# GpSimd's order in an attention period: low halves behind the routing's copy and at step 16, outputs spread over steps 10 to 21

## What is computed

```python
x = _layernorm(x + _L0_attn_ref(x, ...))  # a scan over time and an MLP
x = _layernorm(x + _L0_ffn_ref(x, ...))   # 8 experts, the 2 best of each token
x = _layernorm(x + _L1_attn_ref(x, ...))  # attention, 16 heads of 8, q and k normalised
x = _layernorm(x + _L1_ffn_ref(x, ...))   # 4 experts, each an attention over its own tokens
```

## Time and profile before

| | |
|---|---|
| time, median of 3 runs | 1452.36 us (1451.96 to 1455.44) |
| profiled execution: span from first to last instruction | 1481.8 us (no other time of it is given) |
| PE busy | 1231.5 us, 83% |
| DVE busy | 964.4 us, 65% |
| ACT busy | 734.6 us, 50% |
| POOL busy | 663.4 us, 45% |
| mean granted clock of PE | 0.878 |

### The profile page before, as it was taken

The page is one execution under the profiler, slowest core; times in us unless marked ns, Lnnn a source line. Parts: engine busy times, 40 slices in busy tenths (PEclk is TensorE's granted clock), DMA queues, the critical chain, the costliest instruction groups (busy, mean ns, idle before and its releaser), DMA issues.

```text
span 1481.8 us, 30563 instructions
## 1 busy us (share of the span) xinstructions
PE 1231.5 (83%) x11664; PEld 742.3 (50%) x11664; DVE 964.4 (65%) x2280; ACT 734.6 (50%) x1244; POOL 663.4 (45%) x1054
## 2 busy tenths in 40 slices
PE   5878786567667889999998998999899888988985
PEld 2555575455223344555555554555555455555543
DVE  4787532255357887777776868677777766757534
ACT  3654432233342456665665656556565554553531
POOL 3376342563167454464443626345363432443430
PEclk7998798797665889999998989999999998998978
DMA  9801465561010001101020110101102010110110
GB/s 337 335 21 34 133 184 161 166 181 54 19 29 23 23 2 40 29 16 38 8 44 8 37 32 13 44 4 42 32 14 43 4 42 15 31 39 9 34 35 8
DMA packets 69480, 87.52 MB, mean 59 GB/s; under 512 B 22062, under 2 KB 54104, under 8 KB 65880
## 3 DMA queue, kind: packets, MB, share of 16 engines
q1 hardware_dynamic: 65240, 77.18, 18.0%
q0 software_dynamic: 4096, 8.40, 1.9%
HBM read 52.16 MB, written 32.21 MB: 57 GB/s over the span
## 4 chain that ended last, share of the span: by engine, by line
PE 41%; DVE 28%; SPq 7%; ACT 7%; issue 6%; POOL 5%; DMA 3%; another core or an unknown queue 2%; ACTq 0%; DVEq 0%; POOLq 0%
PE ps L1677 19%; DVE mneg_e L1492 8%; PE ps L1757 7%; PE ps L864 5%; PE ps L1780 3%; DVE mneg_l L1492 3%; SPq L1141 2%; PE ps L960 2%; SPq L1137 2%; DVE q L1547 1%; PE ps L972 1%; SPq L1159 1%; POOL q_low L1224 1%; PE ps L1777 1%
## 5 line engine op out<-in xcount | busy, mean ns | idle before, releaser
L1335 ACT ACTIVATE probs<-ps 128x1024 f32<-128x1024 f32 x384 | 390.0, 1024 | 260.8 <-PE ps L1677 257.2
L1492 DVE TENSOR_REDUCE mneg_e<-ps 128x2 f32<-128x512 f32 x512 | 337.1, 685 | 66.1 <-PE ps L1677 63.1
L1677 PE MATMUL ps<-k_high,q_high 32*128 32x256 f16 x1024 | 164.3, 286 | 51.0 <-DVE mneg_e L1492 41.1
L1492 DVE TENSOR_REDUCE mneg_l<-ps 128x2 f32<-128x512 f32 x256 | 167.8, 682 | 57.3 <-PE ps L1677 56.1
L1757 PE MATMUL ps<-probs,v_e 128*32 128x256 f32 x2048 | 141.6, 395 | 8.2 <-ACT v_e L1360 4.7
L1677 PE MATMUL ps<-q_high,k_high 32*128 32x256 f16 x1024 | 142.1, 278 | 4.0 <-ACT probs L1335 3.3
L1677 PE MATMUL ps<-q_low,k_high 32*128 32x256 f16 x1024 | 141.4, 275 | 0.0
L1677 PE MATMUL ps<-q_high,k_low 32*128 32x256 f16 x1024 | 140.3, 273 | 0.0
L1677 PE MATMUL ps<-kT,qT 32*128 32x256 f16 x512 | 75.9, 285 | 35.6 <-DVE mneg_e L1492 16.7
L1677 PEld LDWEIGHTS ps<-k_high,q_high 32*128 32x128 f16 x1024 | 54.4, 93 | 97.4 <-DVE mneg_e L1492 62.8
L1288 POOL TENSOR_TENSOR on_e<-o_e,on_e 128x512 f32<-128x512 f32 x60 | 75.7, 1274 | 60.1 <-DMA on_e<-scratch_e 60.1
(11 more groups left out here) (245 smaller groups left out, 2553.6 us busy)
## 6 DMA issues: line engine op xcount, KB each, us to landing
by_expert<-expert_w SPq DMA_DIRECT2D x12, 1536.0 KB, 14.4
expert_w<-in_expert_w SPq DMA_DIRECT2D x48, 321.0 KB
on_e<-scratch_e SPq DMA_DIRECT2D x60, 256.0 KB, 4.8
tokens<-by_expert SPq DMA_DIRECT2D x48, 128.0 KB
by_expert<-y_tokens SPq DMA_DIRECT2D x48, 128.0 KB
on_l<-scratch_l SPq DMA_DIRECT2D x128, 32.0 KB, 1.8
sums_l<-o_l SPq DMA_DIRECT2D x128, 2.0 KB
q_high<-shiftT_e SPq DMA_DIRECT2D x128, 2.0 KB
```

Source lines behind the costliest of these rows:

```text
L1335: act.activation(probs[:, probs_slot(r, i)].rearrange("p j s -> p (j s)"), s_banks(i).rearrange("p j s -> p (j s)"), ACT.Exp, scale=0.5 if ...
L1492: v.tensor_reduce(to, tiles(max_bank(k)), axis=AX, op=ALU.max, negate=True).then_inc(kind.max_used, 1)
L1677: return pe.matmul(o, l, r, start=start, stop=stop)
```

## The change

GpSimd's conditions are put in another order. In period `r`, the low halves of groups 2 and 3 of sequence `r` move from step 5 (both of group 2), 6 and 7 to step 6 behind the copy `routeT16` (both of group 2), step 7 (`q` of group 3) and step 9 (`k` of group 3). The low halves of group 1 of sequence `r + 1` move from steps 20 and 21 to step 16, ahead of `on_l`. The four multiplications `on_e` move from steps 9, 10, 11 and 12 to steps 10, 13, 17 and 21. SP waits at steps 4 and 9 for the low halves of the two groups whose `q_high` row it is about to write. DVE takes `inverse_l` at step 13, no longer at step 12. No operation is added or left out.

```diff
--- before.py
+++ after.py
@@ -1154,6 +1154,7 @@
                     if i in (4, 9) and valid(r):
                         b, part = r, i // 9
                         sp.wait_ge(E.shiftT_ready, 2 * b + part + 1)
+                        sp.wait_ge(s.q_low_ready, G * b + 2 * part + 2)
                         for j in range(J):
                             row = ROW * j + SHIFT_E
                             sp.dma_start(q_high[row:row + 1, b % 2, 2 * part:2 * part + 2], shiftT_e[2 * j:2 * j + 2, :])\
@@ -1259,30 +1260,30 @@
                         pool.memset(v_e[:], 1.0).then_inc(pool1_ready, 1)
                     if i == 0:
                         round_k(r, 3)
-                    if i == 5:
-                        rest_of_q(r, 2)
-                        rest_of_k(r, 2)
-                    if i == 6:
-                        rest_of_q(r, 3)
-                    if i == 7:
-                        rest_of_k(r, 3)
                     if i in (11, 14, 17, 22):
                         round_q(r + 1, (11, 14, 17, 22).index(i))
                     if i in (12, 15, 20):
                         round_k(r + 1, (12, 15, 20).index(i))
-                    if i in (13, 20):
-                        rest_of_q(r + 1, (13, 20).index(i))
-                    if i in (14, 21):
-                        rest_of_k(r + 1, (14, 21).index(i))
+                    if i in (13, 16):
+                        rest_of_q(r + 1, (13, 16).index(i))
+                    if i in (14, 16):
+                        rest_of_k(r + 1, (14, 16).index(i))
                     if i == 17 and valid(r + 5):
                         root_steps(r + 5)
                     b = r + 1
                     if i == 6 and valid(b):
                         pool.wait_ge(s.routeT_ready, b + 1)
                         pool.tensor_copy(routeT16[0:ROUTE], routeT[:, b % 4, :]).then_inc(s.route16_ready, 1)
+                    if i == 6:
+                        rest_of_q(r, 2)
+                        rest_of_k(r, 2)
+                    if i == 7:
+                        rest_of_q(r, 3)
+                    if i == 9:
+                        rest_of_k(r, 3)
                     b = r - 1
-                    if i in (9, 10, 11, 12) and through_memory(b):
-                        g = i - 9
+                    if i in (10, 13, 17, 21) and through_memory(b):
+                        g = (10, 13, 17, 21).index(i)
                         if g == 0:
                             pool.wait_ge(E.inverse_landed, J * DMA * (b + 1))
                         pool.tensor_tensor(on_e[:, :, g], o_e[:, :, g], on_e[:, :, g], ALU.mult).then_inc(E.on_ready, 1)
@@ -1622,7 +1623,7 @@
                         v.tensor_tensor(qk, qk, rqk[:].unsqueeze(2).broadcast_to([P, 2 * T * H, HD]), ALU.mult)\
                             .then_inc(s.qn_ready, 1)
                     b = r + 2
-                    if i == 12 and valid(b):
+                    if i == 13 and valid(b):
                         v.wait_ge(L.sums_landed, 2 * J * DMA * (b + 1))
                         if b > 0:
                             v.wait_ge(L.inverse_stored, DMA * b)
```

## The result

The changed kernel takes 1429.12 us (median of four runs, 1420.32 to 1430.42), the kernel before 1452.16 us on the same chip (four runs, 1445.73 to 1455.44). The ratio is 0.9842, 95% interval 0.9805 to 0.9879: 22.9 us faster. The forecast was a faster kernel at 1439 us: the direction was right, and 23 us stand where 13.4 were summed up.

A forecast was written before the change was run, and what follows sets the result against it. PE was taken to set the pace, losing time where it waits for DVE. Terms of -3.1, -5.6, -6, +8.2, -2.4 and -4.5 us summed to -13.4 us, from 1452.4 to 1439 us for the median; range 1424 to 1461 us.

The forecast's parts named there:

- Step 1: DVE's three comparisons no longer wait for GpSimd, ending 1.6 us earlier; PE gains 0.22 us in 14 periods, -3.1 us.
- The clock: Behind the waits of steps 22 and 2, three of 22 falls to 1.2 GHz go, -4.5 us (bounds 0 and -33).
- the prediction's own sign of being wrong: The clock falls at another place of the period than before, for instance behind the new gap at step 16.
- rival B: Much faster, around 1424 us: the clock stays up at both places, half of the 22 falls gone; chance 0.10.
- Step 4: `o_e` and `sums_e` come earlier, so `inverse_e`'s four long stalls go; half of -11 us taken, -5.6 us.
- `inverse_l`: Taken at step 13, not 12, it ends DVE's wait for `sums_l` and PE's gaps behind it, -6 us.
- The lock at step 15: L1618 on DVE waits for GpSimd's `q_low`; PE idles 0.91 us in nine more periods, +8.2 us.
- The fourth `on_e`: At step 21, ahead of L1622: over in time, it spares PE's 0.48 us; -2.4 us, between -4.8 and +8.
- 0.23 us: At step 21, the most that an early `q_low` gains of the 1.39 us wait of `q`.
- A: The forecast: step 1 pays at steps 2 and 4, step 15's lock takes some back; 1428 to 1447 us, chance 0.50.

The follow-up runs named there:

- without the late halves: The whole change with the low halves of groups 2 and 3 put back at steps 5, 6 and 7; 1452.87 us, ratio to before 0.9994.
- with the busy DVE: Kernel before with only the low halves of groups 2 and 3 moved, plus eight more DVE comparisons behind the three of step 1; 1455.88 us, ratio 1.0026.
- the kernel at step 17: The whole change with the low halves of group 1 at step 17 instead of step 16; 1433.34 us, ratio to before 0.9834.
- the late halves alone: Kernel before with only the low halves of groups 2 and 3 moved behind the routing's copy, with SP's wait; 1424.79 us, ratio 0.9787.

## Why the prediction was right in sign and short in size

*Step 1, right.* -3.1 us were taken, 0.22 us in 14 periods, since ACT's `weight` copy does not move. It did not: it starts 2.15 us after the first comparison in both kernels (1050.54 - 1048.39 before, 1018.55 - 1016.40 after). PE's projection starts 3.20 us after that comparison instead of 3.45. That is 0.25 us; in six of the 13 periods that have this projection the start was later still before (3.60 to 4.07), and over all 13 it is 5.8 us, within the bounds given (0 and -9.7).

*The clock, the term that was far too small.* "I count three of the 22 falls as gone, -4.5 us." Of the 14 behind step 2, 13 are gone, and of the eight of step 21 one; new ones stand at step 4, nine instead of five. No fall of these periods lies at a new place, the prediction's own sign of being wrong. The 13 projections of step 2 took 44.5 us together, 2.8 to 3.78 each, and now 26.6, 2.05 each: -17.9 us, near the prediction's own price of 1.52 us for each fall. That is rival B's mechanism at one of its two places, and B had a chance of 0.10. PE's matmuls at step 2 are not only small ones, as the argument against B had it: the projection is the work that the fall slows. The direct loss and the loss by the clock have one cause, and the second is three times the first; the kernels without the late halves and with the busy DVE show both come back together.

What did PE do before the clock fell? It waited 0.68 us or so behind the comparisons' step, ahead of the projection; with 0.51 us there, the clock mostly stays. The sum of the waits does not decide. In three periods of the changed kernel PE also waits 0.72 to 0.86 us ahead of the comparisons' step (0.86 in the timeline above), with the 0.51 more than the 0.32 and 0.69 of before, and the clock stays. With the longer wait two of the small matmuls of the scores also stand behind it and no longer ahead of it. Whether the length of the wait or this order decides is not shown. The Trainium skill, "TensorE: Matmul & The Clock Gate" (section on the second failure mode), says that short idles of PE between groups of matmuls can be enough to send its clock to and fro between the two levels. This case's traces agree: with waits of 0.65 us or more ahead of the projection the clock fell in 76 of 78 periods of six kernels, with 0.51 in 6 of 91 of seven.

*Step 4, wrong.* "The four long stalls at step 4 (0.82 us in the row) should go", -5.6 us. They stayed: 3.5 us of waiting over six times, 3.6 over six before. `o_e` starts 1.15 us after the first comparison instead of 2.82, 1.7 us earlier as forecast, and SP's eight loads with it. But DVE reaches `inverse_e` earlier by as much, because the projection between them is 1.5 us shorter: from `o_e` to `inverse_e` it is 6.93 us (7.09 before). The step moved one end of the wait and held the other. Moving `inverse_e` itself a step took the stall away.

*`inverse_l`, wrong in time.* The wait went as described, and PE's waits for `mneg_l` shrank; the -6 us did not come. Alone the move gives 1.0011, and taken out of the change 0.9854 for 0.9842. Counting a gap on PE as gained was the error. Where the time goes instead is open: alone, GpSimd waits longer for `on_l`, but in the whole change it does not (14.4 us, 20.1 before).

*The lock at step 15, right.* L1619 takes 1.08 us and PE loses 0.80 us in ten periods, 8.0 us; the kernel before paid 0.91 of it in its one instance, so +7.1 us, where +8.2 was taken. That is a sum of PE's gaps: alone the part costs 6.2 us (1.3 to 11.3), and the kernel at step 17, without the lock, is not to be told from the whole change. The Trainium skill, "SBUF — State Buffer" (section on the two separate sides), lets the first of the two engines keep the shared pair for its whole instruction; the row bears it out, 1.08 us beside a `q_low` of 1.15. The rows add that one DVE operation, L1618, gets through between `k_high` and `q_low`, which stand back to back.

*The fourth `on_e`, right, but for a reason that lies in step 16.* -2.4 us were taken. In the whole change PE's gap behind L1623 is nil in seven of eleven periods and 0.27 to 0.40 in four, against 0.47 in eleven: -3.9 us. The spread does not earn it: put back, L1623 takes 0.70 us too, and alone it costs 13.9 us. The "0.23 us" for `q_low` was right for the order of before and no measure of the move, since the four parts are not independent. Alone they give -31.0, +1.6, +13.9 and +6.2, together -9.3 us; all four in one kernel give -22.9.

Sum with what was measured (step 1, projections of step 2, lock, L1623; step 4 and `inverse_l` at nothing): -5.8 - 17.9 + 7.1 - 3.9 = -20.5 us, within the interval of the result (-17.6 to -28.3). It is no proof, since the new falls at step 4 are not in it. But its three terms that are waits of PE come to -2.6 us together, and PE's idle time in the stage says much the same, -3.1 us. The gain is PE's busy time: 27.8 us less than in the long profiled execution of before, 18.9 less than in the kernel without the late halves.

*Luck.* The time lies inside A's range, 1428 to 1447 us, at its edge. It got there because two terms that did not come (step 4 and `inverse_l`, -11.6 us) made up for most of what the clock's term lacked at step 2 (-17.9 for -4.5).

*Open.* Why the clock falls at step 4 nine times in the whole change and four times with the late halves alone is not explained by their gaps there, which are alike (0.99 us, and 1.3 us or more in a stall).

## What to carry to other kernels

When an engine waits at a place that the clock falls behind, price the wait with the work that runs behind it at half clock: here some 0.4 us of waiting carried 1.4 us. Compare PE's busy and idle time over the same work, too: a busy time that shrinks with the same matmuls shows a gain that no wait shows. Test each part of a reordering alone and taken out, because one part can carry the gain and two others only pay for each other. Where a DVE operation waits for a load, moving that operation a step later took the wait away both times here (`inverse_e`, `inverse_l`), and gave time only once; moving its producer earlier did not, since both shifted alike.

## What was unexpected

A wait of PE of 0.68 us (longer in a few periods), once in a period of 60 us, was followed by 1.2 GHz in 12 or 13 of 13 periods in each of the five kernels with the lock at step 1, and one of 0.82 us in 13 of 13 in the kernel with the busy DVE. Where 0.51 us stood in its place, in seven kernels, the clock fell in none to two of 13. During those stretches PE counts as busy for the whole window (2.00 of 2.00 us at 0.50), so its busy share alone does not show the loss. And eight comparisons of 128x32 on DVE, 1.77 us in 60, cost 2.3 us a period.
